# Transposing the normalized tokens of six groups by DMA from ACT's queue in place of TensorE and VectorE

## What is computed

```python
h = _L0_tok_ref(x)                                   # (16, 250, 64)
h = h + attn(_layernorm(h), Wq, Wk, Wv, Wo)          # 8 heads, softmax replaced by sigmoid
h = h + ffn(_layernorm(h), ...)

# attn
qkt = jnp.einsum('bifh,bjfh->bijh', q, k)
attn = jax.nn.sigmoid(qkt * SCALE)
out = jax.nn.relu(wv @ Wo)
# ffn
all_out = _experts_mlp(x, eW1, eb1, eW2, eb2, eW3, eb3)     # 4 experts, 64 -> 128 -> 64 -> 64
shared = _shared_mlp(x, sW1, sb1, sW2, sb2, sW3, sb3)       # 64 -> 64 -> 128 -> 64
gates = jax.nn.softmax(x @ gW + gb, axis=-1)
topv, topi = jax.lax.top_k(gates, 2)
topw = jax.nn.softmax(topv, axis=-1)
```

## Time and profile before

| what | value |
|---|---|
| time, median of 3 runs | 165.88 us (162.79 to 167.39) |
| the profiled execution | 163.06 us |
| its span, first to last instruction | 161.3 us |
| PE busy | 150.9 us (94%) |
| ACT busy | 113.0 us (70%) |
| DVE busy | 108.9 us (68%) |
| POOL busy | 54.5 us (34%) |
| mean granted TensorE clock | 0.974 |

### The profile page before, as it was taken

The page is one execution under the profiler, slowest core; times in us unless marked ns, Lnnn a source line. Parts: engine busy times, 40 slices in busy tenths (PEclk is TensorE's granted clock), DMA queues, the critical chain, the costliest instruction groups (busy, mean ns, idle before and its releaser), DMA issues.

```text
span 161.3 us, 6648 instructions
## 1 busy us (share of the span) xinstructions
PE 150.9 (94%) x2824; PEld 91.4 (57%) x2824; DVE 108.9 (68%) x278; ACT 113.0 (70%) x155; POOL 54.5 (34%) x101
## 2 busy tenths in 40 slices
PE   7999695999999999999999999999999999999990
PEld 2478532454466576666656454634757565775780
DVE  2497998998768867676674849776469784444440
ACT  3598982977888998989796989467445728457430
POOL 4000019686798772746244161717000000000000
PEclk9999569999999999999999999999999999999998
DMA  4380000175895756746575200000010100101002
GB/s 117 92 260 0 4 0 0 66 191 133 253 252 140 231 155 165 222 124 202 166 223 143 59 4 4 4 0 0 4 34 4 34 13 23 30 6 36 18 21 59
DMA packets 13185, 14.09 MB, mean 87 GB/s; under 512 B 1244, under 2 KB 12416, under 8 KB 13092
## 3 DMA queue, kind: packets, MB, share of 16 engines
q1 hardware_dynamic: 12576, 13.22, 29.3%
q10 hardware_dynamic: 580, 0.45, 0.9%
HBM read 9.06 MB, written 4.60 MB: 85 GB/s over the span
## 4 chain that ended last, share of the span: by engine, by line
PE 67%; DVE 11%; ACT 9%; DMA 7%; issue 3%; SPq 1%; POOL 0%; DVEq 0%; POOLq 0%
PE ps L449 13%; PE ps L467 13%; PE ps L569 9%; PE ps L587 7%; PE ps L630 7%; PE ps L478 5%; DMA y_stage<-YP 4%; PE ps L597 3%; DMA YS<-y_stage 3%; PE ps L614 2%; ACT probs L1196 2%; PE ps L317 2%; ACT area L1131 2%; ACT square L1129 1%; PE ps L503 1%
## 5 line engine op out<-in xcount | busy, mean ns | idle before, releaser
L1196 ACT ACTIVATE probs<-ps 125x1000 f32<-125x1000 f32 x64 | 61.7, 1008 | 9.6 <-PE ps L449 6.6
L467 PE MATMUL ps<-probs,xn 124*32 124x250 f32 (+1 forms) x512 | 39.2, 375 | 0.0
L449 PE MATMUL ps<-YS,XT 128*32 128x500 f16 x448 | 34.3, 376 | 0.6 <-DMA YS<-y_stage 0.3
L467 PEld LDWEIGHTS ps<-probs,xn 124*32 124x32 f32 (+1 forms) x512 | 15.7, 109 | 12.4 <-issue 2.1
L1228 ACT ACTIVATE H2r<-ps,wf 128x500 f32<-128x500 f32 x16 | 10.8, 677 | 15.4 <-PE ps L587 15.4
L854 DVE COPY ZS<-ps 128x250 f32<-128x250 f32 x32 | 12.8, 412 | 8.5 <-PE ps L467 8.4
L1058 DVE TENSOR_TENSOR area<-H2r,ps 128x500 f32<-128x500 f32 x16 | 10.8, 673 | 9.0 <-ACT H2r L1228 9.0
L587 PE MATMUL ps<-area,wf 128*64 128x500 f32 x64 | 16.7, 585 | 0.0
L1214 ACT ACTIVATE area<-ps,wf 128x500 f32<-128x500 f32 x24 | 15.9, 672 | 0.9 <-PE ps L569 0.9
L449 PEld LDWEIGHTS ps<-YS,XT 128*32 128x32 f16 x448 | 10.6, 96 | 9.1 <-ACT probs L1196 4.6
L835 DVE CAST YP<-ps 128x500 f16<-128x500 f32 x14 | 9.5, 676 | 7.9 <-PE ps L408 7.9
(11 more groups left out here) (158 smaller groups left out, 255.5 us busy)
## 6 DMA issues: line engine op xcount, KB each, us to landing
YS<-y_stage SPq DMA_DIRECT2D x40, 125.0 KB, 3.2
y_stage<-YP SPq DMA_DIRECT2D x10, 250.0 KB, 2.8
YS<-y_stage SPq DMA_DIRECT2D x8, 250.0 KB, 4.4
tower_out<-res SPq DMA_DIRECT2D x7, 124.0 KB
y_stage<-YP SPq DMA_DIRECT2D x6, 125.0 KB, 4.0
wf<-wf_in SPq DMA_DIRECT2D x1, 648.0 KB, 6.0
wa<-wa_in SPq DMA_DIRECT2D x1, 512.0 KB, 5.2
y_stage<-YP ACTq DMA_DIRECT2D x2, 125.0 KB, 2.9
```

What stands on the lines that cost most here:

```text
L449: last = mm(ps[k0:k1, 2 * (n % 2) + j, 0:TG].rearrange("p (h n) -> p h n", h=2), XT[:, g % 3, (2 * bb + cj) * P + k0:(2 * bb + cj) * P + k ...
L467: last = mm(ps[R * hh:R * hh + R, 4 + bb, half * TB:(half + 1) * TB], xn[0:keys, 4 * g + 2 * bb + cj, :], probs[0:keys, n % 3, hh, :], sta ...
L1196: fn(probs[:, n % 3].rearrange("p (j h) n -> p j (h n)", j=2), ps[0:P, 2 * (n % 2):2 * (n % 2) + 2, 0:TG], ACT.Sigmoid, scale=SCORE_SCALE) ...
```

## The change

For groups 0 to 5 (NX = 6) the 16 PE transposes and the DVE copy go. In their place ACT issues one DMA transpose for each group (`x2_turn`), after the activation of step t = 7, in the same place of the group's order in which PE's transposes stood. It reads a whole `x2s` buffer, now 128 partitions by 512 columns, and writes `X2T[:, g]`, now four tiles of 128 columns of which 125 are used. POOL clears the three partitions without tokens once at the start. POOL's wait for a free `x2s` buffer and PE's waits for `X2T` go over to the semaphores of the DMA (`x2_ready`). `gates(0)` stands in step 51 in place of 49, behind `attn_out(5)`, and ACT's two sigmoids for it after step 54 in place of 52. Groups 6 and 7 stay with PE and DVE.

```diff
+NX = NG - 2
-        x2s = sb("x2s", [P, 2, 4, 2 * F], F16)
-        X2T = sb("X2T", [128, NG, TG], F16)
+        x2s = sb("x2s", [128, 2, 4, 2 * F], F16)
+        X2T = sb("X2T", [128, NG, 4, 128], F16)
+        x2t_in = [sem("x2t_in0"), sem("x2t_in1")]
+        def x2_ready(eng, g):
+            if g < NX:
+                eng.wait_ge(x2t_in[g % 2], 16 * (g // 2 + 1))
+            else:
+                eng.wait_ge(x2t_cp, g - NX + 1)
...
@@ PE
                 if g >= 4:
                     pe.wait_ge(h2_done, g - 3)
-                if g >= 5:
-                    pe.wait_ge(x2t_cp, g - 4)
...
-                pe.wait_ge(x2t_cp, 4 * r + 4)
+                for g in (NX - 2, NX - 1, NG - 1) if r else (2, 3):
+                    x2_ready(pe, g)
...
                     else:
-                        pe.wait_ge(x2t_cp, g - 2)
+                        pe.wait_ge(h2_done, g - 1)
                     attn_out(g - 1)
-                if t == 7 and g >= 2:
-                    x2_transpose(g - 2)
-                if n == 8 * (NG - 2) + 1:
+                if n == 8 * (NG - 2) + 3:
                     gates(0)
...
             def layer1(g, e):
                 n = (E + 1) * g + e
+                if e == 0:
+                    x2_ready(pe, g)
...
@@ DVE
                 z_take(g, 2)
-                x2_take(g - 2)
                 squares2(g - 1)
...
@@ ACT
+            def x2_turn(g):
+                if g == 0:
+                    act.wait_ge(x2s_pad, 1)
+                act.wait_ge(x2s_done, g + 1)
+                act.dma_start_transpose(X2T[:, g], x2s[:, g % 2].rearrange("p t c -> p (t c)")).then_inc(x2t_in[g % 2], 16)
...
-                if n == 8 * (NG - 2) + 4:
+                if n % 8 == 7 and 2 <= n // 8:
+                    x2_turn(n // 8 - 2)
+                if n == 8 * (NG - 2) + 6:
                     gate_sigmoids(0)
...
@@ POOL
+            v.memset(x2s[:], 0.0).then_inc(x2s_pad, 1)
...
                 if g >= 2:
-                    pool.wait_ge(x2t_mm, g - 1)
+                    x2_ready(pool, g - 2)
```

30 lines of the change are left out of this document (17 added, 13 removed).

## The result

The changed kernel took 165.36 us (median of 22 runs, 163.23 to 167.00), the kernel before 164.05 us (22 runs, 162.28 to 167.39). The ratio of their runs is 1.0064, with a 95% interval of 1.0036 to 1.0091: slower by 1.0 us by the ratio and by 1.3 us by the medians, which is less than 2% and more than nothing. Timed once more later (e10), it was 1.0086 [1.0050, 1.0121]. The profiled execution of the changed kernel took 165.37 us with a span of 163.5 us, that of the kernel before 163.06 us with 161.3 us.

A forecast was written before the change was run, and what follows sets the result against it. DVE's string was taken to set each group's end, not PE. Terms 0 - 0.1 (step 56) + 0.2 + 0.3 (issue) - 0.13 (gates) + 0.45 (landing) = +0.7, rounded to +0.9 us: 166.8 us, range 163.8 to 171.3.

The forecast's parts named there:

- the landing: Group 3's transpose, issue to landing before `gates(0)`: 5.0 us against 4.55 free, wait 0.45 us; ends 3.2 and 6.7.
- group 6: Issue cost on ACT where activations stand back to back: free up to 0.68 us, at 1.0 us a loss of 0.3.
- the sigmoids' delay: ACT's sigmoids behind step 54, DVE's softmax some 2 us later, delaying `mix(56)`: at most 0.3 us, taken as 0.
- PE's transposes worth nothing: Groups 0 to 3: PE arrives 0.22 us earlier but waits 0.37 us for DVE, not 0.15; gain 0, at most 0.1.
- the cover: DVE's string from `y_project` to `z_take` hides PE's saving; were it 0.2 us shorter, the gain would be 0.9 us.
- The issue (X): Unknown duration of a transpose issue on ACT's queue: taken 1.0 us, ends 0.35 and 2.0; costs 0.2 us in groups 2 to 5.
- the forecast's formula: ACT's next activation starts 0.23 + X + 0.10 us after the one ahead; X up to 1.05 us free in groups 2 to 5.
- Rival A: ACT's queue is blocked by the issue in five groups: at X = 2.0, +6.3 us, 172.2; chance 0.2.
- `gates(0)` behind `attn_out(5)`: On PE the two stand together and gates end at 87.35 against 87.48 us: a gain of 0.13 us.
- The estimate of 5.2 us: Four 128 x 128 blocks in a row at the skill's 1309 ns per DMA block; by that rule speaks against the change.
- Rival B: The transposes hold the DMA engines, so reads of `YS` and `gates(0)` come late: +8 us, 174; chance 0.1.
- Rival C: PE's time comes out because DVE's string shortens along with PE: -1.1 us, 164.8; chance 0.1.

The follow-up runs named there:

- e10: The changed kernel unedited, timed and profiled again: 165.61 us, ratio 1.0086 to the kernel before.
- e1: Kernel before with PE transposes and DVE copies of groups 0 to 5 left out, X2T cleared once instead: 163.94 us, ratio 0.9982.
- e7: Changed kernel with the six DMA transposes issued by SP in place of ACT: 165.81 us, ratio 0.9967 to the kernel before.
- e4: Kernel before without transposes and copies of groups 0 to 5, and with DVE's `z_take(g, 1)` ahead of residual and layer norm: 163.01 us, ratio 0.9917.
- e13: Kernel before with `z_take(g, 1)` ahead of the residual and first router logits and sigmoids two steps later, PE transposes kept: 163.84 us, ratio 0.9968.
- e15: Kernel before with only DVE's `z_take(g, 1)` moved ahead of residual and layer norm, a repeat run: 163.29 us, ratio 0.9926.
- e16: Kernel before with `z_take(g, 1)` moved ahead, logits and sigmoids two steps later, and softmax behind `squares2`: 163.24 us, ratio 0.9953.
- e9: Changed kernel with ACT issuing each of the six transposes a second time, into a spare tile: 176.24 us, ratio 1.0611 to the kernel before.
- e14: Changed kernel with DVE's `z_take(g, 1)` moved ahead of residual and layer norm: 164.98 us, ratio 1.0048 to the kernel before.
- e11: Changed kernel with `z_take(g, 1)` ahead of the residual and softmax behind `squares2`, ACT issuing: 164.65 us, ratio 1.0042 to the kernel before.
- e2: Kernel before with only the first router logits and the two sigmoids two steps later: 165.34 us, ratio 1.0066.
- e5: Kernel before with logits and sigmoids two steps later and DVE's softmax behind `squares2`: 164.17 us, ratio 0.9941.
- e18: Changed kernel, SP issuing, fourth transpose ahead of four loads, `z_take(g, 1)` moved ahead, logits, sigmoids and softmax at their old places: 164.57 us, ratio 1.0021 to kernel before.
- e3: Kernel before with the six DMA transposes from ACT's queue added, into a tile nobody reads: 166.36 us, ratio 1.0130.
- e12: Changed kernel with `z_take(g, 1)` ahead of the residual, softmax behind `squares2`, and SP issuing the transposes: 163.66 us, ratio 0.9972 to the kernel before.

## Why the prediction was right and wrong

The forecast of +0.9 us against a measured 1.0 (1.3 by the medians) looks like a hit, and its nearness is luck: of its terms those for the landing and for group 6 were too large, and those for the first issue and for the softmax too small. The time itself, 166.8 us, was 1.4 above the measured 165.36: it stood on a median of three runs, 165.88, and the median of 22 was 164.05. From 164.05 us to 166.8 would be 1.7%, where 0.64% was measured. Two steps failed in the mechanism: the sigmoids' delay, taken as 0 because it was followed only to the first copy, and the issue, taken as alike in all groups.

*PE's transposes worth nothing: right.* Forecast 0.37 us of wait for DVE at a group's end, found 0.33, of which 0.21 for DVE's copy. The groups of 8.72 us in e1 and e7, where PE's transposes are gone and the copy stays where it was, show it. What was said of the cover isn't right: with it gone the gain was to be 0.9 us, and by e4 against e13, e15 and e16 it is 0.1 us a group, 0.4 in all, since ACT comes next. (A slip with no effect on the sum: the earlier trace rows give 3.2 us for 128 transposes of 218 ns, so nearly nine overlap, not four.)

*The issue (X): mis-sized, above all the first.* Taken as 1.0 us and alike in all groups, 0.2 us for groups 2 to 5. Five issues took 1.21 to 1.25 us, but begin with the activation instead of 0.23 us behind it. The 0.23 us of the earlier trace rows was no property of an issue: that DMA waited for its data, which DVE finished at 38.11 us (start and duration, from DVE's timeline of before):

```profile
37.43 0.68 DVE L842 TENSOR_TENSOR YP<-ps,YP 128x500 f16<-128x500 f32 x1
```

So an X of 1.21 acts as the forecast's formula would with 0.91 to 0.97, and these issues stay near the edge of ACT's slack, as e9 shows by putting a second one there. In group 6, where 0.3 us was forecast, the issue began 0.33 us ahead of its activation (92.98 and 93.31) and the next activation came 0.97 us after it, where it was 1.01 before: no loss. The first issue took 1.40, 1.87, 2.03 and 1.60 us (changed, e10, e14, e11) and the stretch around it 4.5 to 5.0 instead of 3.9 us. That is 0.7 to 1.1 us in one place where the forecast had 0.05, and the largest single difference between the traces of the two kernels (0.9 us). Rival A (X from 1.5 on) described this, but for all groups; it came true in one. Why the first is longer is open: it stands where SP's loads of wide rows are in flight, and on SP's queue it was long as well (1.35 to 2.54 us), where it cost nothing in that stretch.

*`gates(0)` behind `attn_out(5)`: right.* They follow each other without a gap, 87.68 to 89.70, and steps 48 to 56 take 0.14 us less than before (forecast: 0.13 for the gates).

*The landing: forecast 5.0 us with 0.45 of wait.* It took 3.8 us and nobody waited. It isn't safe: the same transpose took 4.2 in e10 and 5.3 in e14, and in e11 `gates(0)` waited 0.52 us. The ends of 3.2 and 6.7 held. The Trainium skill ("Advanced Engine Details and Errata", section "X-Bar Transpose (TRN2)") has a transposing DMA as fast as a regular one; the trace agrees roughly, median 4.3 us from issue to landing against 3.6 for the reads of YS, most of which have as many bytes. 0.6 us of this is the issue, 1.21 us where a read took SP about 0.6 (before). The estimate of 5.2 us from the Trainium skill ("VectorE: DVE Perf Modes", section "The three transpose paths") is too long for five of the six (2.4 to 4.5 us): the last, with little else in flight, was issued and landed within 2.4 us. The first took 7.4.

*The sigmoids two steps later: the step that failed.* I wrote "At most 0.3 us, taken as 0", having followed the late softmax to the first copy behind it, `mix(56)`. That one was harmless, as forecast. The cost lies one more engine on: softmax, `squares2(5)`, POOL's layer norm, its overlap with DVE's short operations, `z_take(7, 1)`, `mix(62)`, which waited 0.61 us. Alone it costs 0.66% by the ratio (e2; 0.1% by the medians), and 0.42% with the group ends repaired (e13 against e15), with intervals that overlap; e5 takes it away by an edit on DVE alone, which shows the way it goes. In the traces it is 0.3 us in the changed kernel and 0.5 in e2 (stretch 63 to `layer1`), so that the bound of 0.3 was near and the 0 was wrong. How the changed kernel's 1.0 us of time divides between this and the first issue isn't settled: the parts overlap, and singly they come to more than the whole.

*Rival B (the transfer holds the DMA engines): not here.* YS landed later (median 3.6 for 3.2 us, 6.6 at most for 4.9), but in the changed kernel no scores of the loop's steady part waited for it. With SP's queue loaded further (e18) they did.

*Rival C (PE's time comes out): not here* (e1, e7). Even where a part of it could come out (e14 against e13, 0.1 us a group) the DMA cost more than it.

Not settled: the changed kernel's stretch 28 to 48 is 0.6 to 1.4 us longer than before's in three profiles; part of it is the moving gap in `attn_out`. And the expert part, from the first `layer1` to the end, is 0.24 us shorter in the changed kernel (60.25 against 60.49 us). The DVE copy of group 5, which stood at its start, isn't the reason: e1 and e4 have no such copy and take 60.49 and 60.51 us.

## What to carry to other kernels

Work taken off the engine on the critical chain is worth what the next arrival at its next meeting point allows; look for the instruction that is waited for there (here a copy that stood behind a layer norm) and move that first: it was worth 0.7% alone, and no version with the transposes on a DMA queue measured better. Then ask what arrives next, since the time freed ends there: of 0.22 us a group only 0.1 was left. A DMA isn't free for the engine that issues it, and a position in a queue is a dependency: price the issue against the slack between two instructions of that engine, for the busiest moment and not the median, and look what stands ahead of it. When a step moves later, follow it through every engine until the wait ends, not to the first consumer.

## What the runs showed that I had not expected

- The issue of a DMA transpose of 128 rows (125 used) by 512 columns of 16 bits kept ACT's queue for 1.21 us and SP's for 1.19 to 1.26 us at best, and up to 2.30 us (e3) and 2.99 us (e18) in places with SP's loads in flight; that the loads make it long wasn't tested. It takes the issuing engine's instruction stream with it: the activation behind it never started sooner than 0.09 us after its end.
- Short DVE operations of 0.2 us took 0.4 to 0.7 us beside POOL's operations on 125x256 elements. In the kernel before one took 0.61 us (at 97.99, beside POOL's 0.61 us at 97.94) and one 0.30, in the changed kernel three took 0.43, 0.63 and 0.60 us.
- In three places a wait cost twice. Behind 3.05 us without work PE's granted clock was 0.64 on average over 4 us, and mixes in e12 took 1.06 us for eight matmuls, at 1.2 GHz, instead of 0.6. Behind the 2.30 us in e9 it was 0.57 from 61 to 65 us, and behind the 2.20 us 0.61 from 105 to 109 us. Behind the 1.39 us in e9 the row of 92 to 96 us still says 1.00.
- PE stops for 0.2 to 1.8 us for no reason that the trace names ("issue"; the longest is e7's at 51.84 us), mostly within `attn_out`, 64 small matmuls that take 0.89 us otherwise. Two profiles of one kernel have 0.48 and 0.22 us in two places, and 0.90 us in one. It may be the supply of instructions, which I didn't test. It is as large as the effect studied, so that one profile of each version is not enough here.
